# Twelve root tiles and four log tiles in the first attention, with GpSimd's shift in another form

## What is computed

```python
q = _l2norm(to_heads(q))          # 16 heads of 8 columns
k = _l2norm(to_heads(k))
cos = jnp.einsum('bhsd,bhtd->bhst', q, k)
g_dist = jnp.arccos(jnp.clip(cos, -1.0 + EPS, 1.0 - EPS))
attn_score = (1.0 + g_dist) ** (-3.2)
n_r = jnp.sum(attn_score, axis=-1)
n_c = jnp.sum(attn_score, axis=-2)
k_tilde = (n_r ** (-1.0))[..., :, None] * attn_score * (n_c ** (-1.0))[..., None, :]
probs = k_tilde / jnp.maximum(jnp.sum(k_tilde, axis=-1, keepdims=True), 1e-12)
out = jnp.einsum('bhst,bhtd->bhsd', probs, v)
```

## Time and profile before

| | us |
|---|---|
| median of 3 runs | 3647.53 |
| lowest and highest | 3646.39 and 3648.2 |
| the profiled execution, its own time | 3644.35 |
| its span, first to last instruction | 3642.6 |
| first attention, from the first head's table load to the last head's end | 116.9 to 1955 |

### The profile page before, as it was taken

How to read it: one execution, slowest core, us unless ns; L and a number is a source line. 1 busy time by engine, 2 the same in 40 slices (tenths; PEclk the granted TensorE clock), 3 DMA queues, 4 the chain that set the end, 5 groups by cost and what they waited for, 6 DMA issues and landing times. The chain is left out here.

```text
span 3642.6 us, 59779 instructions
## 1 busy us (share of the span) xinstructions
PE 3123.6 (86%) x19264; PEld 1306.7 (36%) x19264; DVE 2800.0 (77%) x3981; ACT 3013.6 (83%) x2658; POOL 2666.2 (73%) x1450
## 2 busy tenths in 40 slices
PE   4888888888889888898886968888888888888899
PEld 2322222222222122221222424555555555555547
DVE  7678988889888898888987977787877778787301
ACT  1799999999999999999995846887878878788722
POOL 2698988989889898898973525776777777677600
PEclk8876677766777667776676978999999999999999
DMA  0100000000000000000001450110001110000100
...
DMA packets 59508, 85.46 MB, mean 23 GB/s; under 512 B 9808, under 2 KB 45904, under 8 KB 58960
## 3 DMA queue, kind: packets, MB, share of 16 engines
...
...
## 5 line engine op out<-in xcount | busy, mean ns | idle before, releaser
L1195 POOL TENSOR_TENSOR lo<-pr,hi 128x1024 f16<-128x1024 f32 x384 | 917.3, 2413 | 384.5 <-ACT hi L1321 382.5
L1244 DVE TENSOR_REDUCE mx<-mx_ps 128x1 f32<-128x512 f32 x1024 | 659.8, 683 | 165.3 <-PE mx_ps L1359 161.8
L1336 ACT ACTIVATE pr<-s_ps 128x1024 f32<-128x1024 f32 x512 | 532.3, 1040 | 264.4 <-PE s_ps L1380 235.2
L1321 ACT ACTIVATE hi<-pr 128x1024 f16<-128x1024 f32 x512 | 548.2, 1072 | 0.0
L1359 PE MATMUL mx_ps<-ka,qa 128*128 128x512 f16 x1024 | 385.8, 398 | 141.5 <-DVE mx L1244 116.9
L671 ACT ACTIVATE wt<-wt 128x2048 f32<-128x2048 f32 x256 | 485.0, 1896 | 0.5
L477 POOL TENSOR_TENSOR wt<-base,wt 128x1024 f32<-128x1024 f32 x192 | 459.1, 2391 | 15.1
L662 ACT ACTIVATE wt<-wt,theta_bias 128x10240 f32<-128x10240 f32 (+2 forms) x96 | 464.3, 4837 | 0.9
L1399 PE MATMUL pv_ps<-vh,hi 128*128 128x129 f16 x4096 | 432.9, 222 | 11.2 <-ACT sums L1327 5.8
L1378 PE MATMUL s_ps<-qa,ka 128*128 128x512 f16 x1024 | 396.7, 387 | 35.1 <-issue 22.4
L473 POOL TENSOR_TENSOR base<-base,shift 128x1024 f32<-128x1024 f32 x192 | 364.1, 1897 | 83.7 <-DVE base L527 83.7
...
## 6 DMA issues: line engine op xcount, KB each, us to landing
...
```

The source lines that it names most:

```text
L1195: eng.tensor_tensor(lo[:, i % NHL, :, :], pr_slot(i), hi[:, i % NHL, :, :], ALU.subtract).then_inc(lo_done, 1)
L1244: eng.tensor_reduce(mx4[:, q // NCH, q % NCH:q % NCH + 1], mx_ps[:, q % 2, :], AX.X, ALU.max)\
L1321: eng.activation(hi[:, i % NHL, :, :], pr_slot(i), ACT.Copy).then_inc(hi_done, 1)
L1336: eng.activation(pr_slot(i), s_ps[:, i % 2, :, :], ACT.Exp, scale=SM).then_inc(exp_done, 1)
```

## The change

- `NL` is 4: twelve root tiles (0 to 11) and four log tiles (12 to 15).
- GpSimd's shift is a `tensor_scalar` with two arithmetic operations (add the constant, times one) in place of a `tensor_tensor` that subtracts a broadcast column; the column `shift` is gone.
- Sigmoid and Arctan run on single tiles (four calls each) in place of two pairs and a single one.
- The groups of Ln hold 4, 4, 2, 2, 1, 1, 1 and 1 tiles in place of 5, 4, 3, 2, 1 and 1; `values` goes by the same groups.
- Fold 4 is the last narrow step. The first wide step is close 2, then the log tiles. In the wide part the close of tile j - 2 and not of j - 3 follows raise and fold of tile j. The first two wide chunks take two slots only, and the order of the three slots begins behind them (`TWO`).
- The row sums of the previous head and the first values stand around close 9; before, both stood ahead of close 8.
- The last weighing of the previous head is four single matmuls behind squares 8 to 11, not four in a row behind square 8. The plan's price of a product is 3.75 in place of 4.35.
- TensorE starts the next head behind the weighing of place 9, before behind that of place 11.

```diff
--- before.py
+++ after.py
@@ -29,7 +29,7 @@
 KST = NPART * NPART * HD0
 GEXP = -3.2
 HALF_PI = math.pi / 2
-NL = 5
+NL = 4
 
 GQK = 16.0
 G4 = GQK ** 4
@@ -322,11 +322,11 @@
     B1, K1, K2, K3, KA = K_POLY
     NQ = NT - NL
     RA = 4
-    GROUPS = (0, NL, NL + 4, NL + 7, NT - 2, NT - 1, NT)
+    GROUPS = (0, NL, NL + 4, NL + 6, NL + 8, NL + 9, NL + 10, NL + 11, NT)
     NG = len(GROUPS) - 1
     NM0 = 2 * NT
     NCU = 2 * NQ
-    PAIRS = tuple(range(0, NL, 2)) + (NL,)
+    PAIRS = (0, 1, 2, 3, NL)
     NSG = len(PAIRS) - 1
     RAISE, FOLD, CLOSE = range(3)
 
@@ -334,15 +334,17 @@
     narrow = [(0, RAISE), (0, FOLD), (1, RAISE), (1, FOLD)]
     for j in range(2, RA):
         narrow += [(j, RAISE), (j, FOLD), (j - 2, CLOSE)]
-    narrow += [(RA, RAISE)]
-    wide = [(RA, FOLD)] + [(NQ + j, CLOSE) for j in range(NL)]
-    for j in range(RA + 1, NQ):
-        wide += [(j, RAISE), (j, FOLD), (j - 3, CLOSE)]
-    wide += [(j, CLOSE) for j in range(NQ - 3, NQ)]
+    narrow += [(RA, RAISE), (RA, FOLD)]
+    wide = [(RA - 2, CLOSE)]
+    wide += [(NQ + j, CLOSE) for j in range(NL)]
+    wide += [(RA + 1, RAISE), (RA + 1, FOLD), (RA - 1, CLOSE)]
+    for j in range(RA + 2, NQ):
+        wide += [(j, RAISE), (j, FOLD), (j - 2, CLOSE)]
+    wide += [(j, CLOSE) for j in range(NQ - 2, NQ)]
     R1 = NCH * len(narrow)
     NRING = R1 + 2 * len(wide)
     RS = NRING - 4
-    assert (RS - R1) % 3 == 2
+    TWO = R1 + 2 * ((2 - RS + R1) % 3)
     ring_at = {step: NCH * i for i, step in enumerate(narrow)}
     ring_at |= {step: R1 + 2 * i for i, step in enumerate(wide)}
 
@@ -370,7 +372,7 @@
     def tile_of(p):
         return NQ + p if p < NL else p - NL
 
-    ROOT_US, CHUNK_US, PRODUCT_US, LOAD_US, LAG_US = 0.954, 0.625, 4.35, 1.3, 2.0
+    ROOT_US, CHUNK_US, PRODUCT_US, LOAD_US, LAG_US = 0.954, 0.625, 3.75, 1.3, 2.0
 
     def root_time(g):
         return ROOT_US * g + (LOAD_US if g >= 2 * NQ else 0.0)
@@ -404,7 +406,7 @@
         o_sb = t("o_sb", [P, BANK])
         small = t("small0", [P, NT, 4])
         ident_h = t("ident_h0", [P, P], F16)
-        theta_bias, shift = t("theta_bias", [P, 1]), t("shift", [P, 1])
+        theta_bias = t("theta_bias", [P, 1])
         vb = t("vb", [P, S])
         m_ps = ctx.enter_context(nc.psum_tensor("m_ps", [P, 2, 2 * BANK], F32))
         r_ps = ctx.enter_context(nc.psum_tensor("r_ps", [P, 2, BANK], F32))
@@ -431,7 +433,7 @@
         def slot(r):
             if r < R1:
                 return r_ps[:, r % 2, :]
-            q = (r - R1) % 3 if r < RS else (r - R1 + 2) % 3
+            q = (r - R1) % 2 if r < TWO else (r - TWO) % 3 if r < RS else (r - TWO + 2) % 3
             return m_ps[:, q, :] if q < 2 else pair_ps
 
         def folds(j, n_, w):
@@ -470,8 +472,7 @@
                     for i in range(2):
                         v = folds(j, i, 2 * BANK)
                         eng.wait_ge(ring_read, NRING * h + at + half * (i + 1))
-                        eng.tensor_tensor(v, v, shift[:, 0:1].to_broadcast([P, 2 * BANK]), ALU.subtract)\
-                           .then_inc(shifted, 1)
+                        eng.tensor_scalar(v, v, -K2 * G4 * G4, 1.0, ALU.add, ALU.mult).then_inc(shifted, 1)
                         eng.wait_ge(shifted, NCU * h + 2 * j + i + 1)
                         u = wt[:, j, cols(i, 2 * BANK)]
                         eng.tensor_tensor(u, v, u, ALU.mult).then_inc(cubic, 1)
@@ -492,7 +493,6 @@
             @block.vector
             def _(eng):
                 eng.memset(theta_bias[:, :], 1.0 + HALF_PI)
-                eng.memset(shift[:, :], K2 * G4 * G4)
                 eng.memset(vh[:, :, HD0 + 2:VC], 0.0)
                 eng.memset(vh[:, :, HD0 + 1:HD0 + 2], 1.0)
                 eng.tensor_copy(ident_h[:, :], ident[:, :]).then_inc(const_ready, 1)
@@ -603,26 +603,29 @@
                     folded(h, RA)
                     if not first:
                         finish(h - 1)
+                    closed(h, RA - 2)
                     for j in range(NL):
                         log_tile(h, j)
-                    for j in range(RA + 1, NQ):
+                    raised(h, RA + 1)
+                    folded(h, RA + 1)
+                    closed(h, RA - 1)
+                    for j in range(RA + 2, NQ):
                         raised(h, j)
                         folded(h, j)
-                        closed(h, j - 3)
-                    if not first:
-                        finish_rows(h - 1)
-                    values(h, 0, GROUPS[1])
-                    closed(h, NQ - 3)
+                        if j == NQ - 1 and not first:
+                            finish_rows(h - 1)
+                        closed(h, j - 2)
+                        if j == NQ - 1:
+                            values(h, 0, GROUPS[1])
                     if not last:
                         for x in range(2):
                             stack(h + 1, x)
                     closed(h, NQ - 2)
-                    values(h, GROUPS[1], GROUPS[2] - GROUPS[1])
-                    values(h, GROUPS[2], GROUPS[3] - GROUPS[2])
+                    for g in range(1, NG - 3):
+                        values(h, GROUPS[g], GROUPS[g + 1] - GROUPS[g])
                     closed(h, NQ - 1)
-                    values(h, GROUPS[3], GROUPS[4] - GROUPS[3])
-                    values(h, GROUPS[4], 1)
-                    values(h, GROUPS[5], 1)
+                    for g in range(NG - 3, NG):
+                        values(h, GROUPS[g], GROUPS[g + 1] - GROUPS[g])
 
                 for x in range(2):
                     stack(0, x)
@@ -734,7 +737,7 @@
                     elif r < R1 + 2:
                         eng.wait_ge(m0_read, NM0 * h + NM0)
                     else:
-                        free = R1 if r == R1 + 2 else r - 2 if r <= RS + 1 else r - 4 if r < RS + 3 else RS + 1
+                        free = r - 1 if r < TWO + 2 else R1 if r == TWO + 2 else r - 2 if r <= RS + 1 else r - 4 if r < RS + 3 else RS + 1
                         eng.wait_ge(ring_read, NRING * h + (RS if r == RS else free))
                     if RS < r < RS + 3 and not last:
 
@@ -751,15 +754,20 @@
                                             start=True, stop=True)
                     mm.then_inc(ring_ps, 1)
 
+                def weigh_chunk(h, p, c):
+
+                    k = tile_of(p)
+                    if c == 0:
+                        eng.wait_ge(vh_ready, NT * (h + 1) + p + 1)
+                    return eng.matmul(o_ps[VC * c:VC * (c + 1), :], vh[:, k, :], wt[:, k, cols(c, BANK)],
+                                      start=(p == 0), stop=(p == NT - 1))
+
                 def weigh(h, p):
 
-                    k = tile_of(p)
-                    eng.wait_ge(vh_ready, NT * (h + 1) + p + 1)
                     if p == 0 and not (isinstance(h, int) and h == 0):
                         eng.wait_ge(o_copied, h)
                     for c in range(NCH):
-                        mm = eng.matmul(o_ps[VC * c:VC * (c + 1), :], vh[:, k, :], wt[:, k, cols(c, BANK)],
-                                        start=(p == 0), stop=(p == NT - 1))
+                        mm = weigh_chunk(h, p, c)
                     mm.then_inc(pv_done, 1)
 
                 def turn(h):
@@ -780,8 +788,10 @@
                     for g in range(NM0):
                         if g >= 2:
                             square(h, g)
-                        if g == 8 and not first:
-                            weigh(h - 1, NT - 1)
+                        if 8 <= g < 8 + NCH and not first:
+                            mm = weigh_chunk(h - 1, NT - 1, g - 8)
+                            if g == 8 + NCH - 1:
+                                mm.then_inc(pv_done, 1)
                         for r in range(done, ring_to[g]):
                             ring(h, r)
                         done = max(done, ring_to[g])
```

## The result

| | us |
|---|---|
| before, median of 5 runs | 3646.39 (3641.12 to 3648.2) |
| the change, median of 5 runs | 3667.19 (3661.55 to 3672.4) |
| ratio, with its 95% interval | 1.0061 (1.0046 to 1.0075) |
| the profiled execution of the change, its span | 3666.56, 3664.8 |

The account below looks back on a forecast made before the run. ScalarE's work and VectorE's chain, within a microsecond, were taken as the bound. VectorE's steps to +106.0, last Ln and Exps to +111.9, plus 0.4 gave 112.3 us a head against 114.36: 33 us over 16 heads, 3615 us, range 3582 to 3642.

Parts of the forecast that it names:

- the last weighing: TensorE, among ScalarE's roots: spreading it over squares 8 to 11 removes 0.7 of ScalarE's 0.94 us wait.
- narrow end of +33.9: VectorE's last narrow step ends there: +32.2 plus 2.5 for fold 4, less some 0.8 of waits.
- ScalarE waiting among the roots by more than 1 us: One of the signs listed beforehand that would show the prediction wrong.
- GpSimd's shift: GpSimd, each half tile: the new form takes 1.3 us, where the old took 1.90.
- ScalarE's busy time: ScalarE, per head: fewer Sigmoid and Arctan tiles, more calls; 2.84 us less in sum.
- Arctan's wait: ScalarE, ahead of the second Arctan: its 0.47 us wait for VectorE's log tile goes.
- the two chains: ScalarE's own work and VectorE's steps through a head, said to be within a microsecond of each other.
- close 10's wait: VectorE's tail, between close 10's halves: a wait for TensorE of 1.2 us where 1.68 stood.
- The term for five weighings: TensorE, entering the next head: five weighings, not three, behind its first squares make the third some 0.4 us late.
- The cover of GpSimd: GpSimd, restart to tile 11: its work stays hidden while the shift takes up to 1.57 us.
- the rival in which GpSimd becomes the bound: GpSimd, tile 0 to tile 11: a shift above 1.76 us decides; 3700 us at 1.90; chance 12%.
- The rival of ScalarE as the bound: ScalarE stays the bound as tail waits and values overlap: a head of 110.4 us, 3584 us; chance 20%.

Follow-up runs that it names:

- e1: The change with the previous head's last weighing again four matmuls in a row behind square 8; 3623.67 us, ratio to before 0.9947.
- e4: The kernel before with only its last weighing split into single matmuls behind squares 8 to 11; 3683.38 us, ratio 1.0109.
- e2: The change with 80 more VectorE instructions (waits already satisfied) ahead of its first stack, so its loop begins elsewhere; 3668.97 us.
- e3: e1 with 80 more VectorE instructions (waits already satisfied) ahead of its first stack, so its loop begins elsewhere; 3628.62 us.
- f3: e1 with values of places 0 to 9 made earlier and places 0 and 1 weighed in the wide part, not the tail; 3626.23 us.
- g3: f3 with two more weighings out of the tail: places 0 to 3 weighed in the wide part, place 4 alone ahead of close 11; 3621.24 us.
- g2: e1 with 92 more VectorE instructions ahead of the second attention, moving its loop's beginning there; 3619.31 us, ratio to before 0.9932.

## Why the prediction was wrong

The step that failed is the one on **the last weighing**, in the part on ScalarE: "It is now spread over squares 8 to 11; I take 0.7 us of it as gone." The sum that gave 112.3 goes by VectorE's chain, and there the same saving is the term "less some 0.8 of waits that came from the undivided weighing" in the narrow end of +33.9. The four matmuls' 1.07 us was divided by four as if they followed each other. They don't: each writes another 32 rows of `o_ps`, and they run side by side. One of them holds TensorE for 0.98 us, so four apart hold it for 3.9 where four together hold it for about 1.0. A price for each change between float32 and float16 matmuls can't stand in for this: from one matmul to four the time grows from 0.98 to 1.00 us (931.69 to the next row at 932.69 in the kernel before), and from four to 28 it grows by 0.22 us each (6.22 us). ScalarE's waits there came to 3.26 us where 0.24 were left in the sum, and VectorE's copy of `o` to +37.0 and not +33.9. "ScalarE waiting among the roots by more than 1 us" stood in the prediction among the signs of its being wrong, and it is the one that came. What would have warned stood in the earlier trace rows: a weighing matmul at 0.22 us on average in float32, no dearer than the float16 ring chunks (two in 0.44 us at 936.90), though the trace has two records of each. No row in which one stood alone was looked for, and the kernel before has none. The Trainium skill (TensorE: Matmul & The Clock Gate, section Part 3: Packing small matmuls) says that matmuls which fill only a part of the array run concurrently when each has its own tile of it, and that the tile's columns go by the output's first partition; e1 and e4 agree, with 1.07 us for four and 1.04 for one.

By the prediction's own steps, in us from the head's first table load; e1 is the change without the failed step:

| step | forecast | the change | e1 |
|---|---|---|---|
| GpSimd's shift | 1.3 (1.06 to 2.4) | 1.05 | 1.05 |
| VectorE's first raise | none given (before: +2.5) | +3.5 | +3.7 |
| copy of `o` | +33.9 | +37.0 | +34.6 |
| wide steps begin | +45.8 | +49.1 | +46.8 |
| row sums | +91.1 | +94.3 | +92.0 |
| wait inside close 10 | 1.2 | 2.04 | 1.16 |
| close 11 ends | +106.0 | +110.1 | +106.9 |
| a head (average) | 112.3 | 116.0 | 112.5 |

The rest of the sum stands in the main. ScalarE's busy time in a head's window fell by 2.4 us (112.09 to 109.69; the forecast had 2.84), Arctan's wait went, the two chains met where they were said to, and **with the one part undone a head measures 112.5 against a forecast of 112.3**. That they agree so closely is in part luck. e1 does not have the 0.8 us that the forecast took from dividing, so by the prediction's own terms it should have taken 113.1; up to the end of close 11 it does run 0.7 to 1.0 us behind the forecast, and makes up most of it behind that. The weighing explains 3.44 us of the 3.7 between forecast and change: 2.4 until the copy of `o`, and 0.9 in the tail, where close 10's wait was 2.04 with it and 1.16 without, by the clock's later rise.

The term for close 10's wait had luck in it too. It was worked out from two weighings that took 2.83 us (1021.76). In the kernel before that holds in every second head only; in the next one the same row is

```profile
1136.04 3.64 PE L761 MATMUL o_ps<-wt,vh 128*32 128x512 f32 x16
```

and VectorE waits 2.51 us there and not 1.68. Before, that cost a head 0.2 us (they alternate between 114.25 and 114.45); in the change, whose two chains meet, it costs up to 1.6 (e2).

The term for five weighings behind the next head's squares was 0.4 and is nothing in e1 and e3, where they begin earlier; in f3, where they begin later, it is 0.66. The late first raise was not foreseen; it costs a head nothing that can be measured (112.54 with it in e1, 112.60 without it in e3). The cover of GpSimd held with much to spare, and with it the rival in which GpSimd becomes the bound fell. The rival of ScalarE as the bound, a head of 110.4, did not come: ScalarE waits in every version run, and f3 and g3 did not free it. The slower side was given 12% for GpSimd alone; the mechanism that came, the weighing's price when it is divided, was in no rival: the range allowed that the 0.8 us "may not come", not that dividing could cost. Two slips change nothing: five tiles at 1.71 us are 8.55 us and not 8.53, and the x56 of the earlier trace rows is 28 matmuls by two records each and not by their weight loads.

Two parts of the time lie outside the steps. Head 0 is 4.3 us shorter than before (115.11 against 119.37), where the sum had 2.06 for every head; it has no weighing of a previous head to divide, and why it gained more than the others would have was not tried. And behind the first attention, in code that is the same, the profiled executions take 3.8 us more than before in the change and 9.5 in e1. That had been taken as fixed. e1's first attention ends 32.7 us earlier than before, against the 33 of the forecast; what came behind it is the main reason why e1 stands at 3623.7 where the forecast was 3615.

Of the versions run, e1, e3, f3, g2 and g3 are faster than both kernels (ratios to before from 0.9932 to 0.9953, and the intervals overlap); e1 is the simplest.
